# A decoder kernel on one core: a third score bank and a new order in the first cross-attention, and exchanged copies in the layer-1 feed-forward

## The chip, the cores and the metric

The kernel runs on one core of a Trainium2 chip. The metric is the device time of one execution in microseconds (us). The engines are PE (matrix multiply, with PEld for its weight loads), DVE (vector), ACT (activations), POOL (GpSimd) and SP, whose queue issues DMAs.

## The reference

A decoder of four layers, each with self-attention, cross-attention and feed-forward, and after each a residual sum and a layer norm; the input has 4 sequences of 512 tokens of width 512. Two of the twelve parts are touched:

```python
def _L0_xattn_ref(q, k, v):            # q: (4, 512, 512); k = v = ctx_512: (4, 512, 128)
    qh = q.reshape(B, S, 8, 4, 16).transpose(0, 2, 3, 1, 4)     # 8 key heads, 4 query heads on each
    kh = k.reshape(B, S, 8, 16).transpose(0, 2, 1, 3)
    vh = v.reshape(B, S, 8, 16).transpose(0, 2, 1, 3)
    scores = jnp.einsum('bkgsd,bktd->bkgst', qh, kh) / 4
    weights = jax.nn.softmax(scores, axis=-1)
    out = jnp.einsum('bkgst,bktd->bkgsd', weights, vh)
...
def _L1_ffn_ref(x, w_gate, w_up, w_down):
    intermediate = jax.nn.silu(bitlinear(x, w_gate)) * bitlinear(x, w_up)
    return bitlinear(fwht(intermediate), w_down)
# bitlinear: activations rounded to 8 bits by their token's largest value, weights to -1, 0, 1
# fwht: Walsh-Hadamard transform over the 2048 intermediate values
```

## The kernel before

The 2048 tokens are 16 tiles of 128. The kernel is a row of stages, one for each part (`l0_attn`, `l0_xattn`, `l0_ffn`, ...). At the start of a stage every engine waits for all engines and DMAs of the stage before. Within a stage each engine has its own function (`tensor`, `scalar`, `vector`, `gpsimd`, `loads`) which walks the same written order and issues its share of each item. Engines run in order; between them there are counting semaphores (`wait_ge`, `done`). `Banks` is a ring of PSUM banks: `take` lets PE wait until the reader of the bank's former content is done.

**First cross-attention (`l0_xattn`).** Scores need nearly full precision, so queries and keys are split into three bf16 parts each, and six products of parts stand side by side in 6 x 16 = 96 rows of one bf16 matmul. `prep` (DVE, POOL) makes the key parts of one context block in `kst`, `prep2` transposes them on PE, and ACT copies them to `KS`. `qsplit` makes a tile's query parts on POOL, `qt` transposes them (2 x 16 transposes, through the banks of the first scores), and ACT copies them to `QS`. Then, per tile, 16 steps:
- `first`: two heads' scores (queries on the partitions) in a double bank of `S1`; DVE reduces them to negated maxima (`MX`). After the 16th step `maxparts` splits these into three bf16 parts, `maxrows` transposes them, DVE copies them to `MT`, and SP sends them by DMA into rows 96 to 98 of `QS`.
- `second`: the scores again, keys on the partitions, four heads at once, now with the maxima rows times the ones in rows 96 to 98 of `KS`, so that the result is score minus maximum. It lands in a bank of `S2`, and ACT writes its exponential to `PT`. The second scores run LAG = 20 steps behind the first.
- `pv`: four narrow f32 matmuls of `PT` with the values and a column of ones, into the output bank `OB`; after four of them ACT copies the bank (L848). `back` turns it (L210) and DVE divides (L883, L886); `over` adds the residual and normalises.

The order of one step n, in the kernel before: `first`, then `qsplit` at j = 3, `qt` at 13 and 14, `maxparts` at 15, then `maxrows`, two `second`, and `pv`, `back`, `over` at distances 1, 3 and 5 behind `second`. Rows 96 to 127 of `QS` are set to zero by POOL at the start, and the second scores multiply all 128 rows.

In the profile, L205 is a matmul and L210 a transpose of any stage; L867 is the reduction of a first score, L841 the exponential, L826 and L834 the copies of the keys and queries, L901 the zeroing of `QS`, L917 to L931 the query split, L680 to L688 a three-part split on DVE, L876 the copy of the maxima, L250 and L266 (and L256, L259 on POOL) the normalisation.

**Layer-1 feed-forward (`l1_ffn`).** A skewed pipeline over the tiles: in round t, `quant` works on tile t, `turn` on t-1, `up` on t-2, `hadamard` on t-3, `stats`, `scale` and `clip` on t-4, `down` on t-5. PE issues hadamard, down, up, turn. DVE and POOL do the transform's last four levels as butterflies (both L1723); DVE takes the maximum (L1847) and clips (L1860). ACT copies the Hadamard results (L1785, L1789), scales and rounds (`scale`, L1794), applies silu (L1780), converts (`clip`, L1799), and copies the transposes for the down projection (`down`, L1809). DVE multiplies gate and up (L1834) and adds the residual (L1865).

## Time and profile before

| | us |
|---|---|
| median of 3 runs | 4958.34 (4950.70 to 4960.86) |
| the profiled execution | 4954.01 |
| its span | 4952.8 |
| PE busy | 4361.0 (88%) |
| PEld busy | 2293.1 (46%) |
| DVE busy | 2905.5 (59%) |
| ACT busy | 1972.0 (40%) |
| POOL busy | 1693.7 (34%) |
| mean granted clock of PE | 0.947 |

The span goes from the first to the last instruction. The first cross-attention takes it from about 422 to 1009 us, the layer-1 feed-forward from about 1980 to 2346 us. Overlapping matmuls count as busy to their modelled end, so a busy PE isn't a full one.

### The profile page before, as it was taken

The numbers are of one execution on the slowest core, as the hardware profiler recorded it, in microseconds if no ns is written. First come the engines' busy times: TensorE is split into PE (matmuls) and PEld (weight loads), VectorE is DVE, ScalarE is ACT, GpSimd is POOL, SyncE is SP. The second block draws the span as 40 slices with busy tenths as digits, with TensorE's granted clock in tenths as the row PEclk, the third lists the DMA queues.
The fourth block names the chain that finished last, engine by engine and source line by source line (L and its number), as shares of the span: only waits on it lengthen the run. The fifth ranks groups of instructions, "written<-read, shape, count | busy, mean of one in ns | idle before, by whom it ended". The sixth has DMA issues, their size and how long they took to land. (4 is left out here: it accounts for less than half of the span.)

```text
span 4952.8 us, 64586 instructions
## 1 busy us (share of the span) xinstructions
PE 4361.0 (88%) x21326; PEld 2293.1 (46%) x21326; DVE 2905.5 (59%) x6493; ACT 1972.0 (40%) x4364; POOL 1693.7 (34%) x1846
## 2 busy tenths in 40 slices
PE   7996888899999988887899989759999998898688
PEld 6773222234445554554333333335555554343466
DVE  5875777668875987786256656633333332556522
ACT  1111676622112324665466777412211221455422
POOL 1324222101112974454011214455555554212411
PEclk9997999999999999998899999879999999999899
DMA  4330000020000001100012211049999987200000
GB/s 141 96 99 22 2 1 2 2 92 1 0 1 1 1 11 52 66 1 10 25 39 58 67 37 23 22 118 229 235 236 235 215 203 157 88 1 18 3 15 20
DMA packets 154394, 327.34 MB, mean 66 GB/s; under 512 B 25969, under 2 KB 39793, under 8 KB 152498
## 3 DMA queue, kind: packets, MB, share of 16 engines
q1 hardware_dynamic: 106370, 222.24, 13.7%
q0 software_dynamic: 46976, 100.56, 10.3%
q8 instruction: 176, 2.88, 0.3%
q14 instruction: 152, 1.25, 0.1%
q10 hardware_dynamic: 720, 0.40, 0.0%
HBM read 377.65 MB, written 79.30 MB: 92 GB/s over the span
## 5 line engine op out<-in xcount | busy, mean ns | idle before, releaser
L205 PE MATMUL ps<-arena 128*128 128x128 f32 (+17 forms) x17068 | 3813.4, 460 | 321.7 <-ACT arena L1809 51.3
L205 PEld LDWEIGHTS ps<-arena 128*128 128x128 f32 (+6 forms) x17068 | 1772.5, 168 | 2143.4 <-issue 1135.5
L210 PE MATMUL ps<-arena 128*128 128x128 f32 (+2 forms) x3234 | 420.2, 269 | 231.6 <-DVE arena L266 59.4
L210 PEld LDWEIGHTS ps<-arena 128*128 128x128 f32 (+2 forms) x3234 | 341.4, 139 | 428.0 <-issue 216.0
L2957 POOL DMA_INDIRECT moe_y<-arena x191 | 305.5, 1599 | 302.4 <-DVE arena L2926 239.5
L256 POOL TENSOR_SCALAR arena<-arena 128x1 f32<-128x1 f32 x160 | 51.9, 324 | 1035.2 <-DVE arena L250 959.6
L2497 DVE CUSTOM_DVE_ANT_0 arena<-ps,arena 128x384 f32<-128x384 f32 (+3 forms) x512 | 220.6, 487 | 281.9 <-PE ps L205 281.8
L867 DVE TENSOR_REDUCE arena<-ps 128x2 f32<-128x1024 f32 x256 | 303.8, 1218 | 86.3 <-PE ps L205 85.6
L2463 ACT ACTIVATE arena<-arena 128x384 f32<-128x384 f32 (+3 forms) x512 | 280.9, 550 | 165.0 <-DVE arena L2497 165.0
L2909 DVE SCALAR_TENSOR_TENSOR arena<-ps,arena 128x128 f32<-128x128 f32 x382 | 103.6, 313 | 410.2 <-ACT arena L2896 410.2
L2896 ACT ACTIVATE arena<-ps 128x192 f32<-128x192 f32 x191 | 63.3, 331 | 689.3 <-PE ps L205 689.3
L841 ACT ACTIVATE arena<-ps 128x512 f32<-128x512 f32 x512 | 277.6, 597 | 129.3 <-PE ps L205 126.7
L205 PE MATMUL ps<-r,r 128*128 128x512 f32 x1024 | 249.2, 406 | 26.4 <-DVE r L3202 25.0
L2926 DVE COPY arena<-ps 128x512 f32<-128x512 f32 x191 | 123.1, 686 | 221.6 <-PE ps L205 221.6
L2540 POOL TENSOR_SCALAR_AFFINE_SELECT arena<-arena 128x512 f32<-128x512 f32 x128 | 82.6, 648 | 464.3 <-ACT arena L2454 463.6
L205 PEld LDWEIGHTS ps<-r,r 128*128 128x128 f32 x1024 | 198.7, 195 | 75.7 <-DVE r L3202 26.7
L2950 POOL DMA_INDIRECT arena<-moe_x,arena x191 | 189.5, 992 | 118.8 <-PE ps L210 76.4
L1723 POOL TENSOR_TENSOR arena<-arena 128x1024 f32<-128x1024 f32 x64 | 164.5, 2590 | 166.9 <-DVE arena L1723 165.7
L353 DVE MAX8 arena<-arena 128x8 f32<-128x512 f32 x304 | 211.2, 695 | 10.4
L351 DVE MATCH_REPLACE8 arena<-arena 128x512 f32<-128x512 f32 x304 | 205.3, 675 | 0.0
L2454 ACT ACTIVATE arena<-ps 128x1024 f32<-128x1024 f32 (+3 forms) x256 | 165.4, 698 | 60.8 <-PE ps L205 60.8
L2684 ACT ACTIVATE arena<-arena 128x128 f32<-128x128 f32 (+3 forms) x256 | 140.4, 549 | 82.7 <-DVE arena L2712 82.4
(319 smaller groups left out, 4080.9 us busy)
## 6 DMA issues: line engine op xcount, KB each, us to landing
arena<-in_L_ffn_gu SPq DMA_DIRECT2D x191, 768.0 KB
arena<-in_L_ffn_dn SPq DMA_DIRECT2D x191, 256.0 KB
arena<-in_L_ffn_dn SPq DMA_DIRECT2D x191, 128.0 KB
arena<-in_L_ffn_w SPq DMA_DIRECT2D x64, 256.0 KB
moe_y<-arena SPq DMA_DIRECT2D x34, 256.0 KB
arena<-in_L_ffn_w_gate SPq DMA_DIRECT2D x32, 256.0 KB
arena<-in_L_ffn_w_up SPq DMA_DIRECT2D x32, 256.0 KB
arena<-in_L_ffn_w_down SPq DMA_DIRECT2D x32, 256.0 KB
```

What stands on the lines that cost most here:

```text
L205: return self.nc.tensor.matmul(out, lhsT, rhs, start=start, stop=stop, skip_group_check=True)
L210: return self.nc.tensor.transpose(out, in_, ident[0:n, 0:n])
L351: nc.vector.match_replace(k.tw, k.tm8, k.tw if j else s, -3.0e38).then_inc(*(dve.done() if j else dve.done("tfree", n)))
L353: nc.vector.max(k.tm8, k.tw).then_inc(*dve.done())
L841: nc.scalar.activation(PT[v][:, t4].rearrange("p h n -> p (h n)"), S2.of("s2", i, j), ACT.Exp).then_inc(*act.done("p", i, j))
L867: nc.vector.tensor_reduce(MX[:, i % 2, 2 * j:2 * j + 2], S1.of("s1", i, j), AX.X, ALU.max, negate=True).then_inc(*dve.done("mx", i, j))
L1723: return f(o[:, :, 0 if op == ALU.add else 1, :], v[:, :, 0, :], v[:, :, 1, :], op)
L2454: nc.scalar.activation(PT[n % 4][:, 2 * j:2 * j + 2, :], S.of("s2", n, j)[:, :, 0:512 - q0], ACT.Exp).then_inc(*act.done("p", n, j))
L2463: nc.scalar.activation(s, s, ACT.Exp, bias=MX[:, i % 2, g, t4:t4 + 1], scale=-1.0, accum_out=ZS[:, i % 2, g, t4:t4 + 1]).then_inc(*act.don ...
L2497: nc.vector.tensor_tensor_reduce(SR[h % 8][:, 0:keys], S.of("s1", n, g // 2)[:, g % 2, 0:keys], MASK[:, 512 - keys:512], -1.0, 3.0e38, ALU ...
L2950: nc.gpsimd.indirect_dma_start(XG[n % NX], None, XD, bass.IndirectOffsetOnAxis(ap=TT[:, n:n + 1].bitcast(U32), axis=0)).then_inc(rows_in[n ...
L2957: nc.gpsimd.indirect_dma_start(YD[n % 2], bass.IndirectOffsetOnAxis(ap=TT[:, n:n + 1].bitcast(U32), axis=0), YG[n % 4], None, compute_op=A ...
```

## The change

In `l0_xattn`:
- `S2` has three banks (4 to 6) instead of two; `OB` has one (7) instead of two.
- In a step, the first of the two `second` comes ahead of `first`; `pv`, `back` and `over` come one step later.
- `second` multiplies 99 rows instead of 128. The zeroing of rows 96 to 127 of `QS`, and SP's wait for it, are gone; rows 96 to 127 of `kst` are set to one in one piece.
- The query split is a function; for tile 0 DVE executes it, at the head of the order ahead of the key preparation; for the others POOL, as before.

In `l1_ffn`, ACT's list has `down` ahead of `scale` instead of behind it.

```diff
--- before.py
+++ after.py
@@ -706,19 +706,22 @@
     OT = [k.alloc([4, P]) for _ in range(2)]
     rz = k.alloc([2, 32])
     oa = [k.alloc([512]) for _ in range(2)]
-    S1, S2, OB = k.banks(0, 2, 2), k.banks(4, 2), k.banks(6, 2)
+    S1, S2, OB = k.banks(0, 2, 2), k.banks(4, 3), k.banks(7, 1)
     LAG = 20
     kv = kst[:, :, 0:96].rearrange("p h (r d) -> p h r d", d=16)
     qv = qst.rearrange("p h (r d) -> p h r d", d=16)
 
     def order():
+        yield "qsplit", 0, 0
         for t4 in range(4):
             yield "prep", 0, t4
             yield "prep2", 0, t4
-        yield "qsplit", 0, 0
         yield "qt", 0, 0
         yield "qt", 0, 1
         for n in range(16 * NT + LAG + 11):
+            i, j = divmod(n - LAG, 16)
+            if 0 <= i < NT:
+                yield "second", i, 2 * j
             i, j = divmod(n, 16)
             if i < NT:
                 yield "first", i, j
@@ -736,15 +739,14 @@
                 yield "maxrows", i, 0
             i, j = divmod(n - LAG, 16)
             if 0 <= i < NT:
-                yield "second", i, 2 * j
                 yield "second", i, 2 * j + 1
-            i, j = divmod(n - LAG - 1, 16)
+            i, j = divmod(n - LAG - 2, 16)
             if 0 <= i < NT and j % 2:
                 yield "pv", i, j // 2
-            i, j = divmod(n - LAG - 3, 16)
+            i, j = divmod(n - LAG - 4, 16)
             if 0 <= i < NT and j in (7, 15):
                 yield "back", i, j // 8
-            i, j = divmod(n - LAG - 5, 16)
+            i, j = divmod(n - LAG - 6, 16)
             if 0 <= i < NT and j == 15:
                 yield "over", i, 0
 
@@ -755,11 +757,31 @@
     def loads():
         for b in range(4):
             dma.start(sp, CX[:, 4 * b:4 * b + 4, :], ins["ctx_512"][b].rearrange("(t p) d -> p t d", p=P), "ctx", b)
-        sp.wait_ge(pool, "qs0")
         for i in range(NT):
             sp.wait_ge(dve, "mr", i)
             sp.wait_ge(pe, "pv", i - 3, 7) if i >= 3 else None
             dma.start(sp, QS[i % 3][96:99, :, :], MT[i % 2][0:96, :], "mrow", i)
+
+    def qsplit(unit, by, i):
+
+        part = [qv[:, :, r, :] for r in range(6)]
+        sc, res = (a.rearrange("p (h d) -> p h d", d=16) for a in (qsc, qres))
+        by.wait_ge(pool if i > 1 else dve, "qparts", i - 1)
+        unit.tensor_scalar(qsc, k.X[:, i, :], 0.25, 1.0, ALU.mult, ALU.mult).then_inc(*by.done("qsc", i))
+        by.wait_ge(by, "qsc", i)
+        by.wait_ge(pe, "qt", i - 1, 3) if i else None
+        unit.tensor_copy(part[0], sc).then_inc(*by.done("qhi", i))
+        by.wait_ge(by, "qhi", i)
+        unit.tensor_tensor(res, sc, part[0], ALU.subtract).then_inc(*by.done("qr1", i))
+        unit.tensor_copy(part[1], part[0]).then_inc(*by.done())
+        unit.tensor_copy(part[4], part[0]).then_inc(*by.done())
+        by.wait_ge(by, "qr1", i)
+        unit.tensor_copy(part[2], res).then_inc(*by.done("qmid", i))
+        by.wait_ge(by, "qmid", i)
+        unit.tensor_tensor(res, res, part[2], ALU.subtract).then_inc(*by.done("qr2", i))
+        unit.tensor_copy(part[3], part[2]).then_inc(*by.done())
+        by.wait_ge(by, "qr2", i)
+        unit.tensor_copy(part[5], res).then_inc(*by.done("qparts", i))
 
     def tensor():
         for what, i, j in order():
@@ -772,7 +794,7 @@
                 t.then_inc(*pe.done("kt", i, j))
             elif what == "qt":
                 s1 = S1.take("qt", i, j, by=((act, "q", i, 2 * j + 1),))
-                pe.wait_ge(pool, "qparts", i)
+                pe.wait_ge(pool if i else dve, "qparts", i)
                 for u in range(2):
                     bb = s1[:, u, :].bitcast(BF16).rearrange("p (h n) -> p h n", n=P)
                     for h in range(8):
@@ -794,7 +816,7 @@
                 v, t4 = tile(j)
                 bb = S2.take("s2", i, j, by=((act, "p", i, j),))
                 pe.wait_ge(dma, "mrow", i)
-                k.mm(bb, KS[b % 2][:, v, t4 * P:t4 * P + P], QS[i % 3][:, 4 * v:4 * v + 4, :].rearrange("p h n -> p (h n)"), True,
+                k.mm(bb, KS[b % 2][0:99, v, t4 * P:t4 * P + P], QS[i % 3][0:99, 4 * v:4 * v + 4, :].rearrange("p h n -> p (h n)"), True,
                      True).then_inc(*pe.done("s2", i, j))
             elif what == "pv":
                 j, t4 = divmod(j, 4)
@@ -850,7 +872,9 @@
     def vector():
         former = -1, 0
         for what, i, j in order():
-            if what == "prep":
+            if what == "qsplit" and i == 0:
+                qsplit(nc.vector, dve, 0)
+            elif what == "prep":
                 dve.wait_ge(dma, "ctx", i)
                 dve.wait_ge(pool, "kst0")
                 if former[0] >= 0:
@@ -891,15 +915,9 @@
                 k.norm(i)
 
     def gpsimd():
+        nc.gpsimd.memset(kst[:, :, 96:128], 1.0).then_inc(*pool.done("kst0"))
         for buf in VA:
             nc.gpsimd.memset(buf[:, :, :, 16:32], 1.0).then_inc(*pool.done("ones"))
-        nc.gpsimd.memset(kst[:, :, 96:128], 0.0).then_inc(*pool.done("kst00"))
-        pool.wait_ge(pool, "kst00")
-        nc.gpsimd.memset(kst[:, :, 96:99], 1.0).then_inc(*pool.done("kst0"))
-        pool.wait_ge(pool, "kst0")
-        for buf in QS:
-            nc.gpsimd.memset(buf[96:128, :, :], 0.0).then_inc(*pool.done("qs0"))
-        pool.wait_ge(pool, "qs0")
         for what, i, j in order():
             if what == "prep":
                 pool.wait_ge(dma, "ctx", i)
@@ -910,25 +928,8 @@
                 pool.wait_ge(dve, "kparts", i, j)
                 for dst, src in ((2, 0), (3, 1), (5, 0)):
                     nc.gpsimd.tensor_copy(kv[:, :, dst, :], kv[:, :, src, :]).then_inc(*pool.done("kparts", i, j))
-            elif what == "qsplit":
-                part = [qv[:, :, r, :] for r in range(6)]
-                sc, res = (a.rearrange("p (h d) -> p h d", d=16) for a in (qsc, qres))
-                pool.wait_ge(pool, "qparts", i - 1)
-                nc.gpsimd.tensor_scalar(qsc, k.X[:, i, :], 0.25, 1.0, ALU.mult, ALU.mult).then_inc(*pool.done("qsc", i))
-                pool.wait_ge(pool, "qsc", i)
-                pool.wait_ge(pe, "qt", i - 1, 3) if i else None
-                nc.gpsimd.tensor_copy(part[0], sc).then_inc(*pool.done("qhi", i))
-                pool.wait_ge(pool, "qhi", i)
-                nc.gpsimd.tensor_tensor(res, sc, part[0], ALU.subtract).then_inc(*pool.done("qr1", i))
-                nc.gpsimd.tensor_copy(part[1], part[0]).then_inc(*pool.done())
-                nc.gpsimd.tensor_copy(part[4], part[0]).then_inc(*pool.done())
-                pool.wait_ge(pool, "qr1", i)
-                nc.gpsimd.tensor_copy(part[2], res).then_inc(*pool.done("qmid", i))
-                pool.wait_ge(pool, "qmid", i)
-                nc.gpsimd.tensor_tensor(res, res, part[2], ALU.subtract).then_inc(*pool.done("qr2", i))
-                nc.gpsimd.tensor_copy(part[3], part[2]).then_inc(*pool.done())
-                pool.wait_ge(pool, "qr2", i)
-                nc.gpsimd.tensor_copy(part[5], res).then_inc(*pool.done("qparts", i))
+            elif what == "qsplit" and i:
+                qsplit(nc.gpsimd, pool, i)
             elif what == "over":
                 k.norm_rstd(i)
 
@@ -1765,7 +1766,7 @@
                 t.then_inc(*pe.done("y", i))
 
     def scalar():
-        for what, i in order("hadamard scale down up clip up2 turn quant"):
+        for what, i in order("hadamard down scale up clip up2 turn quant"):
             m = sm[:, i, :]
             if what == "turn":
                 act.wait_ge(pe, "xt", i)
```

## Rows read from the trace of the kernel before

**Rows 1.** Stretches: busy us (x count) of PE, PEld, DVE, ACT, POOL; clock, DMA, GB/s.
```profile
489.00:945.00 456.00, 403.55 (x2427) 132.15 (x2425) 337.59 (x467) 315.97 (x537) 106.22 (x190) 0.98 0.01 2
```

**Rows 2.** Waits in the first cross-attention, 489 to 945 us.
```profile
ACT arena L841 <- PE ps L205: 111.2, 89, 7.6
PEld ps L205 <- ACT arena L841: 85.6, 180, 1.6
...
PE ps L205 <- DMA arena<-arena: 6.6, 6, 1.2
```

**Rows 3.** Groups by shape, 400 to 1020 us.
```profile
L867 DVE TENSOR_REDUCE arena<-ps 128x2 f32<-128x1024 f32 x256 | 303.8, 1218 | 86.3 <-PE ps L205 85.6
...
L205 PE MATMUL ps<-arena 128*128 128x512 bf16 x512 | 173.5, 389 | 26.7 <-ACT arena L841 9.5 <-DMA arena<-arena 6.6
L205 PE MATMUL ps<-arena 96*128 96x512 bf16 x512 | 163.7, 404 | 16.9 <-DVE arena L867 11.0 <-ACT arena L826 2.3 <-ACT arena L834 2.3
```

**Rows 4.** Timeline of PE's weight loads, 497 to 501 us.
```profile
497.13 0.98 PEld L205 LDWEIGHTS ps<-arena 96*128 96x128 bf16 x6 [0.84 <-DVE arena L867]
...
499.13 0.10 PEld L205 LDWEIGHTS ps<-arena 128*128 128x128 bf16 x1 [0.39 <-ACT arena L841]
499.45 0.16 PEld L205 LDWEIGHTS ps<-arena 128*32 128x32 f32 x8 [0.23 <-issue]
500.45 0.55 PEld L205 LDWEIGHTS ps<-arena 96*128 96x128 bf16 x4 [0.84 <-DVE arena L867]
```

**Rows 5.** Timeline of the drain, ACT.
```profile
986.39 2.16 ACT L841 ACTIVATE arena<-ps 128x512 f32<-128x512 f32 x4 [0.72 <-PE ps L205]
...
989.28 2.16 ACT L841 ACTIVATE arena<-ps 128x512 f32<-128x512 f32 x4 [0.72 <-PE ps L205]
```

**Rows 6.** Timeline of the first cross-attention's prologue.
```profile
424.19 10.57 POOL L901 MEMSET arena<- 32x4096 bf16 x3
...
440.38 0.23 DVE L680 CAST arena<-arena 128x128 bf16<-128x128 f32 x1 [1.96 <-PE ps L210]
...
443.81 0.23 DVE L680 CAST arena<-arena 128x128 bf16<-128x128 f32 x1 [2.02 <-PE ps L210]
...
446.19 1.01 PE L210 MATMUL ps<-arena 128*128 128x128 bf16 x8 [2.42 <-POOL arena L912]
...
452.83 3.62 PE L210 MATMUL ps<-arena 128*96 128x128 bf16 x32 [5.63 <-POOL arena L931]
...
457.83 1.86 PE L205 MATMUL ps<-arena 96*128 96x512 bf16 x4 [1.38 <-ACT arena L834]
```

**Rows 7.** Timeline at two tile boundaries, 744 to 779 us.
```profile
746.51 2.35 DVE L867 TENSOR_REDUCE arena<-ps 128x2 f32<-128x1024 f32 x2
...
747.78 0.26 PE L210 MATMUL ps<-arena 128*96 128x128 bf16 x1 [1.92 <-DVE arena L867]
...
778.44 1.22 DVE L867 TENSOR_REDUCE arena<-ps 128x2 f32<-128x1024 f32 x1
```

**Rows 8.** Timeline of one tile of the layer-1 feed-forward; the last row cuts at 2172.
```profile
2163.97 2.08 ACT L1794 ACTIVATE arena<-arena 128x2048 f32<-128x2048 f32 x1
...
2165.95 1.93 ACT L1809 ACTIVATE arena<-ps 128x1024 bf16<-128x1024 bf16 x2
...
2167.02 10.53 PE L205 MATMUL ps<-arena 128*128 128x512 bf16 x48 [2.69 <-ACT arena L1809]
...
2168.94 10.41 POOL L1723 TENSOR_TENSOR arena<-arena 128x1024 f32<-128x1024 f32 x4 [8.86 <-DVE arena L1723]
...
2172.30 2.51 DVE L266 TENSOR_SCALAR arena<-arena 128x512 f32<-128x512 f32 x1
...
2177.59 0.75 DVE L1834 SCALAR_TENSOR_TENSOR arena<-ps,arena 128x512 f32<-128x512 f32 x1 [0.31 <-PE ps L205]
...
2168.94 3.27 POOL L1723 TENSOR_TENSOR arena<-arena 128x1024 f32<-128x1024 f32 x1 [8.86 <-DVE arena L1723]
```

**Rows 9.** Timeline of that stage's end, DVE.
```profile
2339.16 0.52 DVE L266 TENSOR_SCALAR arena<-arena 128x512 f32<-128x512 f32 x1
```

## The prediction

> **What bounds the kernel now.** I read the stretch table first, then waits, groups by shape and the timelines of the two stages that the diff touches. The first cross-attention fills its middle [rows 1], with PE busy on paper for 403.6 of 456 us and DVE for 337.6, so neither is saturated as such. The waits say what ties them: ACT's exponentials wait for PE, and PE's weight loads wait for those same exponentials [rows 2]. That is a ring through two PSUM banks, and the reader should see it in the timeline [rows 4]. Weights of a second score wait until an exponential has freed its bank (499.13, 0.39 us idle), then the P·V block starts (499.45), and the next group starts at 500.45. Two steps take 500.45 - 497.13 = 3.32 us. Without firsts, in the drain, the ring alone takes 989.28 - 986.39 = 2.89 us [rows 5]. One tile of 128 queries has 16 steps and goes from 746.51 to 778.44, 31.9 us [rows 7]: 8 x 3.32 = 26.6, and 5.3 for transposing the next queries, turning the output and the maxima.
>
> The prologue is a serial chain [rows 6]: GpSimd memsets until 434.8, four context blocks at 443.81 - 440.38 = 3.43 us each, the query split on GpSimd (PE idles 5.63 us for it), transposes at 452.83, first score at 457.83.
>
> In the layer-1 feed-forward a tile is a ring as well [rows 8]: ACT does the 2.08 us scale, then two transposed copies (1.93 us), and the down projection waits 2.69 us for them although its transposes were done long before.
>
> **Third bank and new order.** PE's work in two steps: a 512-column bf16 matmul lasts 0.39 to 0.40 on paper [rows 3], but they overlap; back to back 48 of them take 10.53 us [rows 8], a pitch of (10.53 - 0.17)/48 = 0.216, where 0.17 is what the last one lasts beyond its pitch. The two steps hold four first and four second scores, eight such matmuls, 1.73. P·V takes 500.45 - 499.45 = 1.00 [rows 4], and about 0.1 is exposed at the weight switch. Sum 2.84, against 3.32: 0.48 saved if ACT never holds PE back. With three banks a second score waits for the exponential three places back. ACT starts 0.4 after its matmul and does four in 2.16 [rows 5] (a pitch of 0.52), so walked through the new order (one second, first pair, one second) each bank is free 0.3 us or more before it is asked for. Full saving: 8 x 0.48 = 3.8 us a tile, 57 us over 15 tiles.
>
> I don't take all of it, because DVE is next. A reduction has a pitch of about 1.15 us back to back (2.35 for two [rows 7]), so two leave 0.5 us spare of 2.84, where they left 1.0. DVE needs 337.6/456 x 31.9 = 23.6 us a tile [rows 1], 5.2 of them not reductions, and these come in lumps (by the timeline, whose rows are too many to show): 2.1 for normalisation behind 0.7 for the output, up to 2.5 for splitting the maxima, and in two tiles of four twice 1.3 for the next keys. PE waits for such a lump already at the boundary, 1.92 us at 747.78 [rows 7]. The first scores have two double banks, so PE can run ahead of DVE by one reduction at most. Walking one tile with these durations: P·V and scores give 3.8; normalisation takes back 1.1, the query transposes (which share the first scores' banks) 0.6, the output's division, now behind the maxima, 0.4. That leaves 1.7, and 3.1 where the maxima's split meets no GpSimd work. Tiles with keys to prepare keep 0.7 and 2.3, also since their maxima come back by DMA and the first second score waits for that already now [rows 2], and is asked for earlier after the change. Mean 2.0 x 15 = 29 us. Ends: 12 (only the tiles without lumps at half value) and 57.
>
> The drain loses its ring too: per two steps four exponentials at 0.52 pitch, 2.08, plus 0.15 while P·V blocks PE, 2.2 instead of 2.89; over 10 pairs 6.9, less 0.4 because the output block now has a single bank and the copy of it stands between. Gain 6.5 (5 to 8). Inside the tiles the single output bank is free in time: its copy ends about 0.9 us after P·V, and the next P·V comes 1.8 us after.
>
> **99 rows and the prologue.** Rows don't enter the price: matmuls with 96 and 128 rows average 404 and 389 ns [rows 3], and six of both kinds fit their weight loads into 0.98 us [rows 4]. I take 0 for 99 rows; bounds 0 and twice the pitch, a rival below. What it removes is the 10.57 us of memsets [rows 6]. The split of tile 0 moves to DVE, nine operations near the 0.52 us of a 512-element one [rows 9]: 4.7, from 422.7 to 427.4, and on the path, as the context arrives at 425.8. Four blocks follow at 3.43: the last starts at 437.7, its transposes end 3.4 later (446.19 + 1.01 - 443.81), at 441.1. The query parts are there by then, so its transposes start at once, and first score comes 457.83 - 452.83 = 5.0 later, at 446.1. Gain 11.7. Ends: 10.4 if the split queues behind GpSimd's three other memsets (1.3 us), 13 if its copies run at half that price.
>
> The rows show such queueing: the DVE operation at 2172.30 takes 2.51 us, and ends 0.3 after a GpSimd operation does, where the same one takes 0.52 alone [rows 8, 9]. The Trainium skill ("SBUF — State Buffer", Who interferes with whom) says why: DVE copies and tensor_scalars and any GpSimd operation take one shared port pair, and the second to start blocks wholly. By that rule, which the trace agrees with, the moved split could block behind the memsets; the prologue would then gain the 10.4 above.
>
> **Exchanged copies in the feed-forward.** ACT ends the last Hadamard copy at 2164.07. With the transposed copies next, the down projection starts at 2165.05 instead of 2167.02 [rows 8], 1.97 earlier, and the up projection with it. The scale ends 1.9 later, at 2167.9; DVE needs it only after its butterflies, at 2168.8 (GpSimd starts on them at 2168.94), so 0.9 us covers it. Then DVE: clip ends 2170.0, the residual sum no longer waits for PE, and the normalising operation is ready at 2171.7 instead of 2172.3. GpSimd's first butterfly ends at 2168.94 + 3.27 = 2172.21. So it slips through then, and ends near 2172.5 in place of 2174.81. The last gating product starts 1.95 earlier than 2177.59, and so do the next tile's Hadamard transposes: 20.5 - 1.95 = 18.55. A second ring sets a floor: DVE butterflies 4.75, GpSimd 10.41, the maximum and its small operations 3.2, waits 0.3, together 18.7. I take 1.8 a tile, over 14 tiles 25, and 1 at the end, where the second last projection no longer waits for the last scale but PE cools down before the last one: 26. Ends: 11 if the slot before 2172.21 is missed (0.8 a tile), 33 if neither ring binds.
>
> **Sum.** 11.7 + 29 + 6.5 + 26 = 73. The profiled execution took 4954.0 us (span 4952.8 and 1.2 around it): 4881. The median of the runs is 4.3 higher, so 4885.
>
> **Rivals.**
> *DVE keeps most of it* (0.23). The attention's tiles gain 12, the feed-forward misses its slot and gains 11: 10.4 + 12 + 5 + 11 = 38, 4920. For it: DVE's lumps and the one-reduction lead; against: DVE still idles 26% of the middle.
> *The rings were everything* (0.15). Tiles gain near the full 57: 11.7 + 50 + 7 + 30 = 99, 4859. For it: waits for exponentials and PE explain most idle [rows 2]; against: the 0.5 us spare.
> *Slower: 99 rows are a slow shape* (0.04). No matmul or weight load with a row number between 96 and 128 is in the trace. If the 512 second scores streamed at half rate, each would cost 0.216 more, 110 us in all, and the gain of the tiles would be gone as PE is their bound: 110 + 29 lost of 73 gained, about 4995 at worst. It decides from about 0.14 us a matmul.
> *The change does nothing that counts* (0.02): the single output bank or the DMA of the maxima takes the place of the ring at the same 3.32, and prologue and feed-forward are paid back behind. It would need each P·V group to wait 1.9 us longer than worked out.
> Also in the feed-forward: were the scale to end 0.9 us later than worked out, the clip would fall behind GpSimd's first butterfly and lose 2.3; that is within the lower case.
>
> **How the numbers follow.** The sum as worked out (0.56), with its own range 4868 to 4900, is the likeliest: 4885. The range for 8 in 10 goes to most of both other cases, 4858 to 4920. A change under 0.2% (10 us) can't be told from none here. Faster 0.94 (0.56 + 0.23 + 0.15), within 0.2% 0.02, slower 0.04.
>
> **What would show it.** First score near 24 us behind the stage's start instead of 35; groups of weight loads at a distance of about 2.84 us in a tile's quiet steps, no waits of PE for exponentials, new waits for reductions behind the normalisation; tiles near 30 us; 2.2 us pairs in the drain; second scores still at 0.216. In the feed-forward a tile of 18.7 us, PE's wait for the transposed copies near 1, the normalising operation down from 2.5 to about 0.8. A tile near 32 us, or one of 19.7 in the feed-forward, would make me wrong on the cover that DVE gives.

## The result and the profile after

| | before | after |
|---|---|---|
| median | 4954.66 (4950.70 to 4960.86, 4 runs) | 4878.68 (4877.82 to 4886.69, 4 runs) |
| the profiled execution | 4954.01 | 4886.69 |
| its span, its mean granted clock | 4952.8, 0.947 | 4885.4, 0.948 |

The ratio is 0.9848 with a 95% interval of [0.9833, 0.9864]: 76 us by the medians. The spans of the two profiled executions differ by 67.4 us only, as the profiled execution of after is the longest of its four (the others took 4877.8 to 4879.0). All sizes below are differences between the profiled executions. By stages (first to last operation of DVE or ACT) the time comes from two places:

| | before | after | gain | predicted |
|---|---|---|---|---|
| last DVE operation of `l0_attn` to the first reduction | 36.3 | 23.3 | 12.9 | 11.7 |
| tile 0 (distance of first reductions) | 24.1 | 24.2 | -0.1 | 0 |
| tiles 1 to 14 | 462.1 | 447.1 | 15.0 | with tile 15: |
| tile 15, first to last reduction | 26.1 | 22.9 | 3.2 | 29 |
| start of the last reduction to the end of the last operation on a line of `l0_xattn` (drain) | 35.4 | 30.9 | 4.5 | 6.5 |
| `l1_ffn`, whole stage | 363.7 | 331.9 | 31.8 | 26 |
| everything else, with the last DVE operation of `l0_attn` 0.8 later | | | 0.1 | 0 |

The last row is worked out: 67.4 less the sum of the others. The other stages move by -2.3 to +2.0, in both signs.

**First cross-attention.** The stretch table over the middle, columns as in [rows 1]:

```profile
489.00:918.00 429.00, 378.84 (x2375) 135.83 (x2374) 329.52 (x463) 305.04 (x523) 108.63 (x190) 0.96 0.01 2
```

DVE is now busy for 329.5 of 429 us (77%; 74% in [rows 1]). The clock is 0.96 instead of 0.98; that will matter below. The waits over the same stretch:

```profile
ACT arena L863 <- PE ps L205: 94.7, 103, 2.7
...
PEld ps L205 <- ACT arena L863: 54.0, 71, 1.7
...
PEld ps L210 <- DVE arena L891: 43.7, 46, 1.0
```

PE's weight loads waited 180 times for an exponential in [rows 2], and do so 71 times now. DVE's reductions (L891 now) are what holds PE more often in its place; the third row shows it for the weight loads of transposes (L210). Groups by shape, 400 to 975 us:

```profile
L891 DVE TENSOR_REDUCE arena<-ps 128x2 f32<-128x1024 f32 x256 | 301.7, 1219 | 98.6 <-PE ps L205 98.6
...
L205 PE MATMUL ps<-arena 99*128 99x512 bf16 x512 | 178.1, 392 | 11.9 <-DMA arena<-arena 9.2 <-ACT arena L863 2.7
L205 PE MATMUL ps<-arena 96*128 96x512 bf16 x512 | 165.8, 409 | 27.5 <-DVE arena L891 14.2 <-DVE arena L910 8.7 <-ACT arena L856 2.6
L205 PE MATMUL ps<-arena 128*32 128x512 f32 x1024 | 141.6, 626 | 0.1
```

Against [rows 3]: 392 ns for 99 rows where 128 took 389, so the odd row number has no price. PE's idle time before the second scores for exponentials fell from 9.5 to 2.7 us; before the first scores it rose from 16.9 to 27.5, 22.9 of them for DVE's reductions and its division of the output (L910). The wait for the maxima's DMA grew from 6.6 to 9.2. Timeline of PE's weight loads in a quiet part of tile 5:

```profile
597.85 0.16 PEld L205 LDWEIGHTS ps<-arena 128*32 128x32 f32 x8 [0.27 <-issue]
598.85 1.42 PEld L205 LDWEIGHTS ps<-arena 99*128 99x128 bf16 x8 [0.84 <-ACT arena L863]
600.68 0.16 PEld L205 LDWEIGHTS ps<-arena 128*32 128x32 f32 x8 [0.42 <-issue]
601.88 1.43 PEld L205 LDWEIGHTS ps<-arena 99*128 99x128 bf16 x8 [1.03 <-ACT arena L863]
603.73 0.16 PEld L205 LDWEIGHTS ps<-arena 128*32 128x32 f32 x8 [0.42 <-issue]
...
601.91 2.89 PE L205 MATMUL ps<-arena 99*128 99x512 bf16 x16 [0.16 <-DMA arena<-arena]
```

Two steps, from P·V block to P·V block, take 2.83 and 3.05 us; 3.32 before [rows 4], 2.84 predicted. The second interval holds tile 4's first second score, and the last row, from PE's own timeline, shows what made it longer: 0.16 us of waiting for the DMA of the maxima. DVE from the 15th step of tile 4 to that of tile 5:

```profile
589.80 1.22 DVE L891 TENSOR_REDUCE arena<-ps 128x2 f32<-128x1024 f32 x1 [2.02 <-PE ps L205]
...
611.18 0.68 DVE L914 TENSOR_TENSOR arena<-arena 128x512 f32<-128x512 f32 x1
...
613.16 4.61 DVE L891 TENSOR_REDUCE arena<-ps 128x2 f32<-128x1024 f32 x4
619.80 1.22 DVE L891 TENSOR_REDUCE arena<-ps 128x2 f32<-128x1024 f32 x1 [2.03 <-PE ps L205]
```

These 16 steps take 619.80 - 589.80 = 30.0 us. Behind the normalisation (from 611.18) four reductions stand back to back, and between 611 and 620 us PE's weight loads idle 2.2 us for reductions: there PE waits for DVE, as the prediction's walk had it. The drain, timeline of ACT:

```profile
953.04 2.07 ACT L863 ACTIVATE arena<-ps 128x512 f32<-128x512 f32 x4 [0.81 <-PE ps L205]
955.43 2.06 ACT L863 ACTIVATE arena<-ps 128x512 f32<-128x512 f32 x4 [0.33 <-PE ps L205]
957.83 2.06 ACT L863 ACTIVATE arena<-ps 128x512 f32<-128x512 f32 x4 [0.33 <-PE ps L205]
```

A pair of steps takes 2.40 where [rows 5] had 2.89 and I had predicted 2.2: ACT still loses 0.33 once per pair. The prologue, for [rows 6]:

```profile
423.40 0.43 DVE L770 TENSOR_SCALAR arena<-arena 128x512 f32<-128x512 f32 x1
...
426.90 0.41 DVE L784 CAST arena<-arena 128x512 bf16<-128x512 f32 x1
...
429.59 1.01 PE L210 MATMUL ps<-arena 128*128 128x128 bf16 x8 [9.65 <-POOL arena L930]
...
439.80 4.43 PE L210 MATMUL ps<-arena 128*128 128x128 bf16 x40 [2.41 <-POOL arena L930]
...
445.67 1.86 PE L205 MATMUL ps<-arena 96*128 96x512 bf16 x4 [1.44 <-ACT arena L856]
```

The split of tile 0 takes DVE from 423.40 to 427.3, 3.9 us (4.7 predicted), the last key transposes and the query transposes are one group of 40, and the first score starts at 445.67 (446.1 predicted).

**Layer-1 feed-forward.** One tile, for [rows 8]:

```profile
2111.22 1.94 ACT L1810 ACTIVATE arena<-ps 128x1024 bf16<-128x1024 bf16 x2
...
2112.52 10.31 PE L205 MATMUL ps<-arena 128*128 128x512 bf16 x47 [0.94 <-ACT arena L1810]
...
2112.90 4.74 DVE L1724 TENSOR_TENSOR arena<-arena 128x1024 f32<-128x1024 f32 x4
2113.03 2.10 ACT L1795 ACTIVATE arena<-arena 128x2048 f32<-128x2048 f32 x1
...
2117.72 10.73 POOL L1724 TENSOR_TENSOR arena<-arena 128x1024 f32<-128x1024 f32 x4 [7.13 <-DVE arena L1724]
...
2120.30 0.98 DVE L266 TENSOR_SCALAR arena<-arena 128x512 f32<-128x512 f32 x1
...
2128.66 2.27 DVE L1848 TENSOR_REDUCE arena<-arena 128x1 f32<-128x2048 f32 x1
```

PE's wait for the transposed copies is 0.94 instead of 2.69, the normalising operation takes 0.98 instead of 2.51: it slipped through ahead of GpSimd's second butterfly, and ends 0.28 us behind the first. From the last Hadamard copy of one tile to that of the next it is 18.8 us (18.5 to 18.8; before 20.5). The second ring is closed: DVE's butterflies 2112.90 to GpSimd's start 2117.72, 4.82; GpSimd 10.73; 0.21; the maximum and its small operations 3.08 (2109.82 to 2112.90 one tile earlier); together 18.84. What GpSimd's butterflies hold back now is DVE's quantising of a later tile:

```profile
2126.27 2.46 DVE L1828 TENSOR_SCALAR arena<-arena 128x512 f32<-128x512 f32 x1
```

In the kernel before it took 0.43 (at 2180.12). It ends at 2128.73, 0.28 behind GpSimd's last butterfly, and so makes up the 0.21 of the ring; more than that it doesn't cost, since the maximum behind it has to wait for that butterfly anyway.

### The profile page after: what moved, and what is told of

The parts are those of the page before. It is cut to its first block and busy times, and to the rows that moved or that the text cites. A ratio compares the mean times of both kernels' runs of the same rounds, so it can differ in the third digit from the quotient of the medians.

```text
span 4885.4 us, 64559 instructions
## 1 busy us (share of the span) xinstructions
PE 4331.6 (89%) x21308; PEld 2303.5 (47%) x21326; DVE 2906.6 (59%) x6502; ACT 1967.3 (40%) x4364; POOL 1681.4 (34%) x1833
## 3 DMA queue, kind: packets, MB, share of 16 engines
q8 instruction: 176, 2.88, 0.3%
## 5 line engine op out<-in xcount | busy, mean ns | idle before, releaser
L205 PE MATMUL ps<-arena 128*128 128x128 f32 (+20 forms) x17050 | 3778.8, 460 | 282.4 <-DVE arena L2498 33.0
L205 PEld LDWEIGHTS ps<-arena 128*128 128x128 f32 (+7 forms) x17068 | 1777.4, 168 | 2063.3 <-issue 1130.9
L210 PE MATMUL ps<-arena 128*128 128x128 f32 (+2 forms) x3234 | 425.6, 272 | 233.3 <-DVE arena L266 59.5
L210 PEld LDWEIGHTS ps<-arena 128*128 128x128 f32 (+2 forms) x3234 | 346.8, 141 | 431.2 <-issue 192.8
L891 DVE TENSOR_REDUCE arena<-ps 128x2 f32<-128x1024 f32 x256 | 301.7, 1219 | 98.6 <-PE ps L205 98.6
L205 PE MATMUL ps<-r,r 128*128 128x512 f32 x1024 | 249.4, 407 | 26.0 <-DVE r L3203 24.6
```

Source lines behind the costliest of these rows:

```text
L205: return self.nc.tensor.matmul(out, lhsT, rhs, start=start, stop=stop, skip_group_check=True)
L210: return self.nc.tensor.transpose(out, in_, ident[0:n, 0:n])
L891: nc.vector.tensor_reduce(MX[:, i % 2, 2 * j:2 * j + 2], S1.of("s1", i, j), AX.X, ALU.max, negate=True).then_inc(*dve.done("mx", i, j))
```

## The experiments

Each ran beside the kernel before, on the same chip as it. The experiments are spread over three chips, on which the kernel before had medians of 4949.4 to 4950.8 us, so where two experiments are compared as a whole the ratio carries the comparison, and for the parts the profiled executions do. A tile's time is the distance of its first reduction to that of the next tile; tiles are counted from 0.

### Each part alone

`xattn_only` leaves the feed-forward's list as it was, `ffn_only` changes nothing but that list:

```diff
-        for what, i in order("hadamard scale down up clip up2 turn quant"):
+        for what, i in order("hadamard down scale up clip up2 turn quant"):
```

> The cross-attention's part alone; the feed-forward keeps its old list on ACT. By the trace after the change the stage is shorter by about 35 us (first score 12 earlier, tiles 1 to 15 shorter by 18, drain by 5). Theory (the two parts are independent, every stage begins after the one before has ended): 35 us faster than before, 4918 to 4925. Rival (the parts act on each other, for instance through the granted clock): 10 us or more away from that.

> The exchange of down and scale on ACT alone, everything else as before. Theory: the stage falls by the 32 us that the trace after the change shows, 4920 to 4927; feed-forward tiles at 18.5 to 18.8 us, PE's wait for the transposed copies near 1 us a tile, and the normalising operation on DVE through the gap behind GpSimd's first butterfly. Rival (part of the 32 us in that trace came from a luckier granted clock and is gone here): 15 to 25 us faster only, with tiles of 22 to 24 us at a clock below 1.

`xattn_only` 4910.83, ratio 0.9915 [0.9899, 0.9932]; `ffn_only` 4916.70, ratio 0.9928 [0.9911, 0.9944]. The product is 0.9844, the change's ratio 0.9848: the parts add, and neither pays for the other. The stages agree: in `ffn_only` `l1_ffn` takes 332.1, with the first cross-attention as before; in `xattn_only` it takes 360.4 (3.3 less than before with the same code: one long tile fewer, see below), and the attention's tiles 1 to 14 take 447.3, the last one 22.9, as in the change.

### Banks and order

`two_banks` keeps the new order, `old_order` the new banks, `both_undone` neither; rows, memsets and the query split stay changed in all three.

```diff
 two_banks, and in both_undone:
-    S1, S2, OB = k.banks(0, 2, 2), k.banks(4, 3), k.banks(7, 1)
+    S1, S2, OB = k.banks(0, 2, 2), k.banks(4, 2), k.banks(6, 2)
 old_order, and in both_undone:
-            i, j = divmod(n - LAG, 16)
-            if 0 <= i < NT:
-                yield "second", i, 2 * j
...
+                yield "second", i, 2 * j
                 yield "second", i, 2 * j + 1
-            i, j = divmod(n - LAG - 2, 16)
+            i, j = divmod(n - LAG - 1, 16)
...
-            i, j = divmod(n - LAG - 4, 16)
+            i, j = divmod(n - LAG - 3, 16)
...
-            i, j = divmod(n - LAG - 6, 16)
+            i, j = divmod(n - LAG - 5, 16)
```

> The change, but with two banks for the second scores and two for the output as before; the new order stays. Theory A (the bank ring is opened by the order as much as by the third bank: a second score, a first pair, a second score lets each exponential run beside the first pair): tiles lose 0 to 1 us each, the drain goes back to pairs of about 2.9 us; 5 to 20 us slower than the change. Theory B (the third bank is what opens the ring): tiles back at 31 to 32 us, 25 us or more slower than the change.

> The change, but with the old order of a step (first, both seconds, P.V one step behind) and three banks. Theory A (either edit opens the ring): within 6 us of the change. Theory B (both are needed, because with both seconds in a row PE still asks for the bank of an exponential that is not done): tiles near 31 us, 15 us or more slower than the change.

> The change with both the old order of a step and two banks for the second scores (two for the output); the prologue, the 99 rows and the feed-forward stay. Theory (either edit opens the ring, as the two runs before say, and only without both it closes): quiet pairs at 3.31 us and tiles at 31.8 to 36 us as before, the drain at 35 us, so 20 to 25 us slower than the change. Rival (two banks and old order each cost their 8 and 5 us in the stage and no more together): 13 us slower.

| | ratio | tiles 1 to 14 | a tile without keys (tile 12) | last tile | drain | whole attention stage, over the change |
|---|---|---|---|---|---|---|
| before | 1 | 462.1 | 32.0 | 26.1 | 35.4 | (other prologue) |
| both_undone, 4903.03 | 0.9912 [0.9896, 0.9929] | 462.1 | 32.0 | 26.1 | 35.4 | 22.7 |
| old_order, 4888.46 | 0.9878 [0.9862, 0.9895] | 449.1 | 30.9 | 24.6 | 32.5 | 5.2 |
| two_banks, 4890.16 | 0.9883 [0.9866, 0.9899] | 449.3 | 30.6 | 23.9 | 35.7 | 7.9 |
| the change | 0.9848 [0.9833, 0.9864] | 447.1 | 29.8 | 22.9 | 30.9 | 0 |

With both undone the sum of the tiles is that of before to the tenth (single ones differ by up to 1.6 us, tiles 1 and 14), which shows that 99 rows, memsets and the moved split do nothing for it. Either edit alone gives 13 of the 15 us of tiles 1 to 14. The 2 us that the other adds are no more than records of one and the same tile code differ by (see the clock, below); in the quiet tile 12, which takes 29.8 or 29.9 in all of those, it adds 0.8 to 1.1. The stage as a whole says it clear of that: undoing one costs 5.2 or 7.9, undoing both 22.7. They are two ways to loosen the same ring, and the next limit stands close behind it. The drain, where no reduction is left, tells them apart: without the third bank nothing is gained there (35.7), with it alone 2.9, and the order adds 1.6 to that. For `two_banks` the first theory (5 to 20 us above the change) is met by the stage's time and by the median, 11.5 above; for `old_order` (within 6) by the stage's time, not by the median, 9.8 above. `both_undone` came out as its theory said, 24 us above. The timeline of ACT in the drain of `two_banks`:

```profile
962.97 2.16 ACT L863 ACTIVATE arena<-ps 128x512 f32<-128x512 f32 x4 [0.72 <-PE ps L205]
965.85 2.16 ACT L863 ACTIVATE arena<-ps 128x512 f32<-128x512 f32 x4 [0.72 <-PE ps L205]
```

2.88 a pair, the ring of [rows 5] again.

### Rows, memsets and the place of the split

`rows128` multiplies 128 rows again and so needs the zeroing of `QS`; the split stays on DVE. `split_pool` puts tile 0's split back on GpSimd behind the keys and leaves the rest.

```diff
 rows128:
+        pool.wait_ge(pool, "kst0")
+        for buf in QS:
+            nc.gpsimd.memset(buf[96:128, :, :], 0.0).then_inc(*pool.done("qs0"))
+        pool.wait_ge(pool, "qs0")
...
+        sp.wait_ge(pool, "qs0")
...
-                k.mm(bb, KS[b % 2][0:99, v, t4 * P:t4 * P + P], QS[i % 3][0:99, 4 * v:4 * v + 4, :].rearrange("p h n -> p (h n)"), True,
+                k.mm(bb, KS[b % 2][:, v, t4 * P:t4 * P + P], QS[i % 3][:, 4 * v:4 * v + 4, :].rearrange("p h n -> p (h n)"), True,
 split_pool:
-        yield "qsplit", 0, 0
         for t4 in range(4):
             yield "prep", 0, t4
             yield "prep2", 0, t4
+        yield "qsplit", 0, 0
...
-            if what == "qsplit" and i == 0:
-                qsplit(nc.vector, dve, 0)
-            elif what == "prep":
+            if what == "prep":
...
-            elif what == "qsplit" and i:
+            elif what == "qsplit":
                 qsplit(nc.gpsimd, pool, i)
```

> The change, with the second scores over all 128 rows again, and so with the zeroing of rows 96 to 127 of the three query buffers (three memsets of 3.5 us on GpSimd) ahead of everything, and SP's wait for it. Theory A (rows cost nothing in a matmul; the memsets hold back the first key block, and by the shared port perhaps the query split on DVE): tiles unchanged, first score 6 to 11 us later, total 6 to 11 us slower than the change. Theory B (99 rows stream or load faster or slower than 128): a difference of 0.2 us or more in every step, thus 50 us or more either way.

> The change, with tile 0's query split on GpSimd behind the four key blocks again. Theory: the split (6.6 us on GpSimd) lies between the last key block and the first transposes again, while the keys start 4.5 us earlier since DVE is free: first score 1 to 2 us later than in the change, total 0 to 3 us slower. Rival (moving the split is what made the prologue short): first score 5 us or more later.

`rows128` took 4888.62, ratio 0.9867 [0.9851, 0.9883]; from the stage before to the first reduction it needs 32.5 us, 9.1 more than the change. Its timeline at the start:

```profile
427.54 10.87 POOL L922 MEMSET arena<- 32x4096 bf16 x3
...
428.41 2.96 DVE L777 COPY arena<-arena 128x512 bf16<-128x512 bf16 x1
431.28 3.68 DVE L778 COPY arena<-arena 128x512 bf16<-128x512 bf16 x1
434.88 3.81 DVE L780 CAST arena<-arena 128x512 bf16<-128x512 f32 x1
```

The three operations take 10.45 us together, where the change does them from 425.00 to 425.96, and each ends with one of the three memsets: DVE is blocked. The Trainium skill ("SBUF — State Buffer", Who interferes with whom) has the mechanism: a DVE copy in a two-port mode and a GpSimd operation exclude each other wholly, and the one that started first wins. The trace agrees, at 3.5 us a copy. In the kernel before the same three memsets [rows 6] held the key preparation in the same way. The prediction told it as a chain, memsets first and then the keys; the rows show that the first key block had started beside them:

```profile
425.80 1.98 DVE L680 CAST arena<-arena 128x128 bf16<-128x128 f32 x1 [3.21 <-DMA arena<-in_ctx]
...
428.14 3.17 DVE L684 CAST arena<-arena 128x128 bf16<-128x128 f32 x1
...
431.68 3.17 DVE L688 CAST arena<-arena 128x128 bf16<-128x128 f32 x1
```

These casts take 0.23 each in the blocks behind, and the five operations of a block 1.4 us instead of the 9.05 here: 7.7 us lost. Tiles 1 to 14 take 439.4 in `rows128`, no more than with 99 rows.

`split_pool` took 4888.40, ratio 0.9869 [0.9853, 0.9886]; to the first reduction it needs 28.7 us, 5.3 more than the change, where I had expected 1 to 2 and the rival at least 5. PE and GpSimd there:

```profile
439.26 1.01 PE L210 MATMUL ps<-arena 128*128 128x128 bf16 x8 [2.42 <-POOL arena L928]
...
445.91 3.62 PE L210 MATMUL ps<-arena 128*96 128x128 bf16 x32 [5.63 <-POOL arena L784]
```

The 5.63 us for which PE waits is the one of [rows 6]: on GpSimd the split lies wholly behind the last keys. Four profiled kernels now give the prologue in every combination (from the stage before to the first reduction, in us):

| | split on GpSimd | split on DVE |
|---|---|---|
| with the memsets | 36.3 (before) | 32.5 (`rows128`) |
| without them | 28.7 (`split_pool`) | 23.3 (the change) |

The memsets are worth 7.6 with the split on GpSimd, about what the blocked casts lost, and 9.1 with it on DVE; the split's move is worth 3.8 beside the memsets and 5.3 without them. Either pays alone, and together they pay a little more than the sum (12.9 against 11.4). The median of `split_pool` lies 9.7 above the change's, more than 5.3; the two ran on different chips, the intervals of their ratios overlap, and a stage that neither touches differs by 3.1 us between the two profiled executions (`l2_attn` 875.7 and 878.8).

### Is DVE the next limit?

`half_max_after` and `half_max_before` take the maxima over 256 of 512 keys, which shortens each reduction and nothing else. The softmax divides the subtracted value out again, so the result stays what it was.

```diff
-                nc.vector.tensor_reduce(MX[:, i % 2, 2 * j:2 * j + 2], S1.of("s1", i, j), AX.X, ALU.max, negate=True).then_inc(
+                nc.vector.tensor_reduce(MX[:, i % 2, 2 * j:2 * j + 2], S1.of("s1", i, j)[:, :, 0:256], AX.X, ALU.max, negate=True).then_inc(
```

> The change, with the maxima of the first scores taken over 256 of the 512 keys (a reduction of about 0.7 us instead of 1.2; the subtracted value is then the largest of half of the row). It takes about 8 us a tile from DVE and nothing from the others. Theory A (DVE is what limits the tiles after the change): tiles fall from 30 to 36 us to 26 to 29, the total by 40 to 80 us. Theory B (PE, ACT or the rings still limit them): less than 15 us.

> The kernel before, with the same shortened reductions. Theory A (before, the ring of second scores and exponentials sets the quiet steps, and DVE counts only at the boundary of a tile and in the first tile): tiles of 30 to 31 us, 15 to 35 us faster than before, quiet pairs still at 3.31 us. Theory B (DVE limited the kernel before too): the same 40 to 80 us as in the change.

`half_max_after` took 4821.35, ratio 0.9737 [0.9721, 0.9753]: 57 us less than the change. `half_max_before` took 4928.21, ratio 0.9957 [0.9943, 0.9971]: 22 us less than the kernel before. Tiles 1 to 14 give 59.2 (447.1 to 387.9) after and 16.2 (462.1 to 445.9) before. So the same relief is worth between three and four times as much behind the change: before, the ring through PE and ACT held the tiles; now DVE does. The stretch table of the middle of `half_max_after`:

```profile
489.00:850.00 361.00, 343.21 (x2292) 128.69 (x2290) 217.49 (x449) 293.21 (x506) 108.86 (x190) 1.00 0.01 2
```

PE is busy for 95% of it, and the clock is whole. So a part of the 59.2 is the clock, which had fallen for 34 us of these tiles in the change; at half clock that is worth 17 us at most, an estimate, and less by `filler`, below.

### The clock

The change's middle has a granted clock of 0.96. Three stretches of 6 us:

```profile
670.00:676.00 6.00, 6.00 (x42) 2.31 (x40) 4.48 (x9) 4.36 (x8) 0.00 (x0) 1.00 0.00 0
676.00:682.00 6.00, 3.83 (x20) 0.84 (x18) 5.90 (x10) 3.18 (x6) 2.72 (x6) 0.94 0.00 0
682.00:688.00 6.00, 6.00 (x34) 3.05 (x35) 1.41 (x2) 3.52 (x5) 0.00 (x0) 0.50 0.00 0
```

From 676 to 682 DVE works through without a pause, PE only for 3.8 of 6 us; then the clock is at 0.50, which is the lower level of 1.2 GHz, and PE's same work takes longer. From tile 2 to tile 14 the stretches at half clock add up to 34 us in the change, 14 in the kernel before. `filler` keeps PE busy at such places: it computes a first score again, into its own bank.

```diff
+FILL = {1: 2, 10: 2}, {1: 2, 10: 3, 11: 3}
...
-                for u in range(2):
+                for u in (0, 1) + (0, 1) * (FILL[i % 4 >= 2].get(j, 0) if i else 0):
```

`spread` prepares the keys at steps 2 and 11 instead of 1 and 9, away from the normalisation's lump:

```diff
-                if i % 4 >= 2 and i // 4 < 3 and j in (1, 7, 9, 15):
-                    yield "prep" if j in (1, 9) else "prep2", i // 4 + 1, 2 * (i % 4 - 2) + j // 8
+                if i % 4 >= 2 and i // 4 < 3 and j in (2, 7, 11, 15):
+                    yield "prep" if j in (2, 11) else "prep2", i // 4 + 1, 2 * (i % 4 - 2) + j // 8
```

> The change, with some first scores computed again into the same bank before PE signals them (4 more matmuls at steps 1 and 10 of a tile, 6 more at steps 10 and 11 of tiles with keys to prepare), all at places where PE waits for DVE's reductions. Theory A (in the change the granted clock falls for 3 to 7 us behind such waits, and that is what makes tiles 7, 11, 13 and 14 1 to 3 us longer): falls within tiles are gone or fewer, those tiles lose 1 to 3 us each, total 0 to 10 us faster than the change. Theory B (the clock has little to do with it, and the added matmuls are on the path): 0 to 10 us slower.

> The change, with the next keys prepared at steps 2 and 11 of a tile instead of 1 and 9, so behind the copy of the maxima and two steps behind the normalisation. Theory A (the preparation hurts by where it stands: it delays the maxima's DMA, and makes one lump with the normalisation on DVE, through which PE idles and its clock falls): the six tiles that prepare keys fall from 33 to 36.5 us to 31 to 34, total 8 to 15 us faster than the change. Theory B (DVE's total work counts, not its place): within 4 us of the change.

`filler` took 4884.82, ratio 0.9871 [0.9855, 0.9888]. Its granted clock in the middle is 1.00, a single fall of 3.4 us is left, and tiles 7 and 11 take 34.4 and 34.5 instead of 36.5 and 36.3. But quiet tiles take 30.3 instead of 29.8, the last tile 25.5 instead of 22.9, and tiles 1 to 14 446.5. So the falls went away as its first theory had it, and the time did not: what the clock gives back, the filling costs. This prices the falls: about 2 us in each of tiles 7 and 11, and 1.1 and 2.2 in tiles 13 and 14 (31.4 and 32.8 in the change, 30.3 and 30.6 here).

`spread` took 4874.85 (4873.96 to 4875.37), ratio 0.9847 [0.9830, 0.9863]. Tile 7 takes 32.8 instead of 36.5 and tiles 1 to 14 take 442.2, though the clock still falls and one of the falls is now in tile 13 (34.3). The six tiles that prepare keys take 200.4 together, against 206.0 in the change and 204.4 to 207.3 in the four other records whose tiles have the same order, so the place of the preparation counts there; by the time of the whole it can't be told from the change. In four records with one and the same tile code (the change, `xattn_only`, `split_pool`, `pool_half`) tiles 1 to 14 took 444.3 to 447.3, and 439.4 in `rows128`, whose second scores alone differ. The stretches at half clock, from tile 2 on, add up to 31 to 38 us in the four and 21 in `rows128`. That this is why they differ is only argued.

### The two rings of the feed-forward

`pool_half` leaves out GpSimd's last two of four butterflies, the last level of the transform, so its output is another.

```diff
-                butterfly(nc.gpsimd.tensor_tensor, i, 3, ALU.add).then_inc(*pool.done("b3", i))
-                butterfly(nc.gpsimd.tensor_tensor, i, 3, ALU.subtract).then_inc(*pool.done("b3", i))
+                pool.also("b3", i)
```

> The change, with the last level of the feed-forward's transform left out (two of the four butterflies on GpSimd, 5 of its 10.4 us a tile; so the output is not the reference's). Theory A (two rings of nearly the same length hold the feed-forward: DVE and GpSimd with 18.7 us, PE and ACT with 18.5): tiles stay at 18.0 to 18.6 us. Theory B (the ring over GpSimd alone holds it): tiles at 14 to 16 us, and the stage 45 us or more shorter.

`pool_half` took 4867.78 (2 runs), ratio 0.9833 [0.9814, 0.9853]. With about 5 us less on GpSimd per tile, a tile takes 18.5 instead of 18.8; the stage gains 13.1, most of it in an early tile (the second distance of Hadamard copies is 17.9 instead of 22.2) and at its end. The timelines of GpSimd and DVE:

```profile
2086.89 5.79 POOL L1724 TENSOR_TENSOR arena<-arena 128x1024 f32<-128x1024 f32 x2 [11.83 <-DVE arena L1724]
...
2105.41 5.78 POOL L1724 TENSOR_TENSOR arena<-arena 128x1024 f32<-128x1024 f32 x2 [11.81 <-DVE arena L1724]
```

```profile
2100.58 4.75 DVE L1724 TENSOR_TENSOR arena<-arena 128x1024 f32<-128x1024 f32 x4 [0.98 <-ACT arena L1790]
```

Now DVE's butterflies wait for the Hadamard copies, the first ring, and it is just 0.3 us shorter than the second.

## Why the prediction was right, point by point

The median was 4878.68 against 4885, in the likeliest case's own range. But the sum of 73 met the spans' 67.4 by errors that cancel in part: 12.8 us too much for tiles and drain, 7.0 too little for prologue and feed-forward. That it stands even closer to the 76 of the medians is luck, for the profiled execution of after was the longest of its four.

- **Prologue, 11.7.** 12.9. The mechanism is shown by `rows128` and `split_pool`. The split on DVE was priced 0.8 too high (0.52 an operation, with most copies taking 0.27 to 0.49). The remaining memsets, from 423.48 to 425.28, hardly held DVE: the cast beside them took 0.49, later ones of its shape 0.41 and 0.42. The lower end of 10.4 wasn't met.
- **The ring through two banks.** Right, shown by `both_undone`. That a saving of 0.48 a pair is not to be had in full, as DVE is next, is shown by the pair of half maxima. The sign "no waits of PE for exponentials" was met in part only: weight loads waited 71 times where they had waited 180 times.
- **Tiles, mean 2.0, sum 29** (15 times 2.0 is 30). Mis-sized: 18.2. The quiet tiles without keys to prepare were right: 30.2 worked out, 29.8 to 30.0 measured (tiles 4, 8, 12). All nine without keys gained 17.3, where 20 of the 29 were meant for them, from 3.4 in tile 5 to a loss of 0.7 in tile 14. The tiles that prepare keys were to gain 0.7 and 2.3, 9.0 over three pairs, and gained 0.3, 2.4, -0.2, -0.5, -0.8 and -0.3, 0.9 in all. That is 8 of the missing 11. It is no accident of this record: in the four others whose tiles have the same order these six take 204.4 to 207.3, against 206.0 here and 206.9 before. Three causes show in the trace. The first is the clock, about 2 us in tiles 7 and 11, priced by `filler`; my walk took all durations at full clock and didn't ask what a PE that waits for DVE does to its clock. The second cause is the later of a tile's two groups of key transposes, which the order puts at step 15, behind the query transposes at 13 and 14, in the same double banks:

```profile
688.36 1.93 ACT L856 ACTIVATE arena<-ps 96x1024 bf16<-96x1024 bf16 x2 [0.98 <-PE ps L210]
...
690.34 0.45 PEld L210 LDWEIGHTS ps<-arena 128*128 128x128 bf16 x8 [1.20 <-ACT arena L856]
690.34 0.62 PE L210 MATMUL ps<-arena 128*128 128x128 bf16 x8 [0.71 <-ACT arena L856]
```

  The key transposes wait until the query copies end at 690.29. I hadn't walked this wait. PE idles 0.55 to 0.97 there in each of the six tiles, where it idled 0.38 for the division of the output before, so it is worth 2.6 us over the six, and no run took it away. The third is the DMA of the maxima, for which PE idles 0.9 more over these six tiles than before; the walk had named this wait, without a price.
- **99 rows at nothing, tile 0 unchanged, a single output bank.** Right: 392 ns against 389, 24.2 against 24.1, and 0.1 us of idle PE ahead of all 1024 P·V matmuls, in the row shown above. `rows128` has no longer tiles with 128 rows either.
- **Drain, 6.5.** Mis-sized: 4.5, as a pair takes 2.40, not 2.2. The cause, the third bank, is shown by `two_banks`.
- **Feed-forward, 26 (14 times 1.8 and 1).** The mechanism was right to the last step: wait down by 1.75, the slot before GpSimd's second butterfly met, tiles of 18.5 to 18.8 against 18.7. The size came out at 31.8. Nine normal tiles gave 16.3 (1.8 each). The first of the fourteen gave nothing (22.1 and 22.2), and neither did the end. But four tiles had taken 22.0 to 24.0 before instead of 20.5, and take 18.5 to 18.8 now: 15.6 instead of 7.2. The stretch table of before around the longest of them:

```profile
2011.00:2023.00 12.00, 9.63 (x57) 5.39 (x56) 9.59 (x12) 5.32 (x7) 4.06 (x3) 1.00 0.01 1
2023.00:2033.00 10.00, 4.98 (x28) 4.98 (x29) 8.46 (x12) 6.86 (x10) 9.92 (x4) 0.66 0.00 0
2033.00:2047.00 14.00, 10.69 (x59) 5.92 (x59) 10.04 (x14) 6.09 (x7) 5.86 (x3) 0.76 0.00 1
```

  PE waits 6.9 us there until 2028.0, 3.3 until 2039.6 and 2.7 until 2063.0, and the clock is at its lower level for 6.8 us of the second stretch and for 6.8 of the third. The first of these waits and its half clock (0.82 from 1981 to 2000) are in the kernel after too; behind it the clock is 1.00 from 2020 to 2250, where before it fell again in each of the four long tiles and was 1.00 from 2067 to 2229, over the tiles of 20.5. In all ten profiled kernels with the exchanged copies and all of the butterflies every tile behind the first two takes 18.5 to 18.8, and in each of the three without the exchange (`xattn_only` and `half_max_before` beside the kernel before) three or four tiles take 22.0 to 24.0: so the exchange does it. That it does so by the shorter wait is only argued.
- **Rivals.** *DVE keeps most of it* had the tiles at 12, my sum at 29, and they came to 18; but the feed-forward's slot, which it gave up, was met. *The rings were everything* needed a DVE with room; `half_max_after` shows that it has none. *99 rows are a slow shape* fell with the 392 ns; its time was also added wrongly, for 110 lost and the tiles' 29 gone make 5024, not 4995. *The change does nothing that counts* fell with the tiles; the single output bank cost nothing.

What stays open: whether `spread` is better than the change, as their ratios are equal; what decides in which tile the clock falls; and whether the exchange spares the long tiles of the feed-forward by its shorter wait.

## What to carry to other kernels

When a ring between two engines is opened, walk one period with the third engine's lumps in it before you price the gain: here DVE had 0.5 us to spare in each pair, and 57 us on paper became 18. Look too for work that stands beside what you remove: three memsets were worth 7.6 us because DVE's casts waited behind them. Walk the rare kinds of period too (here those that prepare keys), through every buffer that they share, for that is where the estimate failed. Two edits that loosen the same ring (a bank, an order) don't add; run each alone to see which of them a stage needs.

## What the runs showed of the hardware that was not expected

- Three DVE copies of 512 bf16 or f32 elements took 2.96, 3.68 and 3.81 us while GpSimd ran memsets of 3.6 us each (`rows128`), and 0.43, 0.27 and 0.42 without them (the change).
- The granted clock fell to half at 681 us though PE's longest waits since 655 us were 1.37 (at 664.8) and 1.63 (at 679.7), with PE busy 3.8 of the 6 us ahead; recomputing scores at such places kept it at 1.00 and won nothing.
- 99 rows are no slow shape: 392 ns a matmul against 389 with 128.
